# Attention projection stage scheduled in even slots, with the residual rows moved to the output stage

## What is computed

```python
x = L0_attn_x                                    # [16, 1024, 256]
mod = (silu(L0_c) @ L0_wmod).reshape(16, 6, 1, -1)
sa, ca, ga, sb, cb, gb = ...                     # shift, scale, gate, twice
h = _layernorm(x) * (1 + ca) + sa
x = x + ga * attn(h)       # attn(h) = h + softmax(mask(rope(q) @ rope(k).T / 4)) @ v @ Wo + bo
                           # q, k, v = (layernorm(h) * gamma + beta) @ W + b, 16 heads of 16
h = _layernorm(x) * (1 + cb) + sb
x = x + gb * ffn(h)        # 8 experts, 512 rows each, gathered and added back
```

## Time and profile before

| | |
|---|---|
| median of 3 runs | 3242.84 us (3241.46 to 3244.81) |
| the profiled execution: its own time | 3240.84 us |
| its span (first to last instruction) | 3239.1 us |
| projection stage | about 59 to 745 us of the span |
| scores and softmax | about 748 to 2612 us |
| output stage | about 2614 to 2894 us |
| busy: PE, DVE, ACT, POOL | 2817.5, 2278.7, 1765.1, 948.2 us |

### The profile page before, as it was taken

One profiled execution on the slowest core, in us unless ns is written; L12 is line 12 of the kernel. 1 busy time (PEld: TensorE's weight loads), 2 busy tenths in 40 slices (PEclk: granted clock), 3 DMA queues, 4 the chain that ended last, 5 costly groups with the idle time before them and its releaser, 6 DMA issues. The chain is left out here.

```text
span 3239.1 us, 48169 instructions
## 1 busy us (share of the span) xinstructions
PE 2817.5 (87%) x17587; PEld 1353.4 (42%) x17587; DVE 2278.7 (70%) x3286; ACT 1765.1 (54%) x3595; POOL 948.2 (29%) x1174
## 2 busy tenths in 40 slices
PE   1677777775999999999999999999999879975997
PEld 0333333331444444444444444444444347753664
DVE  4899999986777777777777777777777435553231
ACT  1455555550777777777777777777777721111111
POOL 2677777762112221121222211212222100003231
PEclk7888888885999999999999999999999989987999
DMA  2355555547344444445444444444444146663332
GB/s 77 127 192 192 192 192 192 191 156 169 71 97 96 92 93 91 99 100 100 97 94 92 94 91 100 100 100 97 91 94 93 42 188 258 258 230 102 79 103 54
DMA packets 173951, 402.96 MB, mean 124 GB/s; under 512 B 33147, under 2 KB 85792, under 8 KB 157107
## 3 DMA queue, kind: packets, MB, share of 16 engines
q1 hardware_dynamic: 167572, 391.36, 46.0%
q0 software_dynamic: 6144, 8.52, 1.5%
HBM read 240.65 MB, written 161.31 MB: 124 GB/s over the span
## 5 line engine op out<-in xcount | busy, mean ns | idle before, releaser
L962 DVE TENSOR_REDUCE mx<-ps 128x2 f32<-128x1024 f32 (+3 forms) x1216 | 1371.4, 1167 | 396.8 <-PE ps L1050 301.6
L1008 ACT ACTIVATE prob<-ps 128x512 f32<-128x512 f32 (+1 forms) x2560 | 1252.0, 560 | 538.4 <-PE ps L1068 529.7
L1043 PE MATMUL ps<-k_rows,q_rows 96*128 96x512 bf16 (+3 forms) x3072 | 911.2, 332 | 38.1 <-DMA k_rows<-k_parts 31.4
L1068 PE MATMUL ps<-q_rows,k_rows 99*128 99x512 bf16 (+3 forms) x3072 | 907.2, 328 | 14.7 <-ACT prob L1008 6.1
L901 POOL TENSOR_SCALAR_AFFINE_SELECT prob<-prob 128x512 f32<-128x512 f32 x512 | 320.0, 637 | 1451.3 <-ACT prob L1008 1451.3
L1087 PE MATMUL ps<-prob,v_rows 128*32 128x512 f32 (+3 forms) x6144 | 628.2, 496 | 0.0
L1068 PEld LDWEIGHTS ps<-q_rows,k_rows 99*128 99x128 bf16 x3072 | 273.1, 98 | 599.0 <-ACT prob L1008 360.2
L1043 PEld LDWEIGHTS ps<-k_rows,q_rows 96*128 96x128 bf16 x3072 | 290.2, 98 | 268.5 <-DVE mx L962 60.7
L1050 PE MATMUL ps<-mask_b,unit_b 128*128 128x128 bf16 (+2 forms) x1408 | 348.6, 248 | 0.0
L701 PE MATMUL ps<-x_t,w_all 128*128 128x512 f32 x512 | 233.2, 598 | 23.2 <-ACT x_t L582 23.2
L1087 PEld LDWEIGHTS ps<-prob,v_rows 128*32 128x32 f32 x6144 | 134.3, 108 | 245.8 <-ACT prob L1008 122.9
(11 more groups left out here) (154 smaller groups left out, 2745.3 us busy)
## 6 DMA issues: line engine op xcount, KB each, us to landing
k_rows<-k_parts SPq DMA_DIRECT2D x384, 128.0 KB, 7.4
v_ones<-v_st SPq DMA_DIRECT2D x64, 512.0 KB, 9.2
v_rows<-v_ones SPq DMA_DIRECT2D x64, 512.0 KB, 9.3
att<-o_sb SPq DMA_DIRECT2D x128, 256.0 KB, 3.2
att_b<-att SPq DMA_DIRECT2D x16, 2048.0 KB, 9.8
q_parts<-stage SPq DMA_DIRECT2D x128, 192.0 KB, 3.6
k_parts<-stage SPq DMA_DIRECT2D x128, 192.0 KB, 3.2
q_rows<-q_parts SPq DMA_DIRECT2D x64, 384.0 KB, 4.5
```

The lines of the kernel that those rows point to most:

```text
L962: dve.tensor_reduce(dst, src, AX.X, ALU.max).then_inc(a_free, 1)
L1008: nc.scalar.activation(prob[:, (g * NPC + i) % RING, h, 0:w], src, ACT.Exp).then_inc(exp_done, 1)
L1043: ins = pe.matmul(ps[:, at, col:col + w], q[0:ROWS, g, h, i * P:(i + 1) * P], k[0:ROWS, g, h, k0:k0 + w], start=(r == 0), stop=True, skip_ ...
L1068: ins = pe.matmul(ps[:, PS_B + bank(g, n), at:at + w], k[0:AUG, g, h, j * P:(j + 1) * P], q[0:AUG, g, h, q0:q0 + w], start=True, stop=True)
```

## The change

In the projection stage the two steps functions become one counter of even slots, s = -23 to 133, eight to a batch. `batch_at(s, lead)` says which tile or unit a piece of work is at. In slot s = 2n PE makes the product of unit n and in odd slots two tiles of v; DVE runs `multiply(n)` in slot 2n + 1, `combine(n)` in 2n + 2, behind `take_rest(n - 1)`; ACT runs `high(n)` in 2n + 3 and `middle(n)` in 2n + 5, POOL `low(n)` in 2n + 6. First norm, modulation and statistics of h go through at one tile a slot (ACT lead 17, POOL 16, DVE 15); the second norm is spread over six slots (`normed_in`). The shift sa is added by POOL behind its multiplication (new L630), but for batch 0, where DVE still adds it. `xin` and `mods_b` get three buffers, the first norm is made in place in `xin`, `h1` goes. L659, L662 and the store L403 go with their DRAM buffer. The factors `rsx` and `nmx` are kept for all 16 batches. In the output stage x is loaded again (`x_b`) with the a2 row, ACT makes the first norm once more (new L1184), two tiles ahead of its copy to `n_t`, POOL multiplies by a2 and adds x (new L1208, L1210). SP issues gate and bias row first, then attention output, x and a2 row.

```diff
+        RING = 3
...
+        START = -23
+        END = B * T + 6
...
+        def normed_in(s):
+            b, k = batch_at(s, 5)
+            if b is not None and k < 7:
+                yield ((0, 1), (2, 3), (), (4,), (5,), (6,), (7,))[k], b
+        def turned_in(s):
+            return normed_in(s - 1)
...
-            for b in range(2):
+            for b in range(RING + 1):
                 load(b)
-            store_residual(0)
-            load(2)
             for b in range(B):
-                if b + 1 < B:
-                    store_residual(b + 1)
-                if b + 3 < B:
-                    load(b + 3)
+                if b + RING + 1 < B:
+                    load(b + RING + 1)
                 store(b)
...
         def _(dve):
+            def slot(s):
+                n = (s - 1) // 2
+                if s % 2 == 1 and 0 <= n < B * NP:
+                    multiply(n)
+                n = (s - 2) // 2
+                if s % 2 == 0 and 0 <= n - 1 < B * NP:
+                    take_rest(n - 1)
+                if s % 2 == 0 and 0 <= n < B * NP:
+                    combine(n)
...
         def _(act):
+            def slot(s):
...
+                for tiles, b in turned_in(s - 1):
+                    for t in tiles:
+                        copy_x(b, t)
+                n = (s - 3) // 2
+                if s % 2 == 1 and 0 <= n < B * NP:
+                    high(n)
+                if s % 2 == 0 and 2 <= s <= B * T:
+                    for t in (s - 2, s - 1):
+                        copy_v(t // T, t % T)
+                n = (s - 5) // 2
+                if s % 2 == 1 and 0 <= n < B * NP:
+                    middle(n)
+                b, k = batch_at(s, 17)
+                if b is not None:
+                    first_norm(b, k)
+                for tiles, b in normed_in(s):
+                    for t in tiles:
+                        second_norm(b, t)
...
         def _(pool):
+            def modulate(b, t):
+                p, r = b % 2, b % RING
+                if t == 0:
+                    pool.wait_ge(mod_in[r], (b // RING + 1) * DMA)
+                reuse(pool, xt_done, (b - 2) * T + t + 1)
+                pool.wait_ge(h1_done, b * T + t + 1)
+                pool.tensor_tensor(h[:, p, t, :], xin[:, r, t, :], mods[:, r, M_CA1, :], ALU.mult).then_inc(h_mul, 1)
+                if b > 0:
                     pool.wait_ge(h_mul, b * T + t + 1)
-                    pool.tensor_tensor(h1[:, p, t, :], h1[:, p, t, :], mods[:, p, M_A2, :], ALU.mult).then_inc(r_mul, 1)
-                for t in tiles:
-                    pool.wait_ge(r_mul, b * T + t + 1)
-                    pool.tensor_tensor(h1[:, p, t, :], h1[:, p, t, :], xin[:, p, t, :], ALU.add).then_inc(r_done, 1)
+                    pool.tensor_tensor(h[:, p, t, :], h[:, p, t, :], mods[:, r, M_SA, :], ALU.add).then_inc(h_done, 1)
...
+            def slot(s):
+                b, k = batch_at(s, 16)
+                if b is not None:
+                    modulate(b, k)
+                n = (s - 6) // 2
+                if s % 2 == 0 and 0 <= n < B * NP:
+                    low(n)
...
-def phase3(nc, B, L, D, ps, ident, wo, ones3, mods_d, out_bias_d, resid_d, att_d, sum_d, out):
+def phase3(nc, x, ps, ident, wo, ones3, rsx, nmx, mods_d, out_bias_d, att_d, sum_d, out):
...
         def load(sp, b, p):
-            sp.dma_start(att[:, p], att_d[b].rearrange("g p t -> p g t")).then_inc(att_in[p], DMA)
-            sp.dma_start(res[:, p], resid_d[b]).then_inc(res_in[p], DMA)
             sp.dma_start(gate[:, p], mods_d[b, M_GA, :].partition_broadcast(P)).then_inc(small_in[p], DMA)
             sp.dma_start(ob[:, p], out_bias_d[b]).then_inc(small_in[p], DMA)
+            sp.dma_start(att[:, p], att_d[b].rearrange("g p t -> p g t")).then_inc(att_in[p], DMA)
+            reuse(sp, r_done, b * T - T)
+            sp.dma_start(xb[:, p], x[b].rearrange("(t p) d -> p t d", p=P)).then_inc(x_in[p], DMA)
+            sp.dma_start(a2[:, p], mods_d[b, M_A2, :].partition_broadcast(P)).then_inc(x_in[p], DMA)
...
             def work(b, half, p):
                 for t in range(T):
+                    n = b * T + t + 2
+                    if n < B * T:
+                        first_norm(n // T, n % T)
                     act.wait_ge(nt_done, b * T + t + 1)
...
+            def residual(b, t):
+                p = b % 2
+                pool.wait_ge(r_norm, b * T + t + 1)
+                if t == 0:
+                    pool.wait_ge(x_in[p], (b // 2 + 1) * 2 * DMA)
+                pool.tensor_tensor(res[:, p, t, :], res[:, p, t, :], a2[:, p, :], ALU.mult).then_inc(r_mul, 1)
+                pool.wait_ge(r_mul, b * T + t + 1)
+                pool.tensor_tensor(res[:, p, t, :], res[:, p, t, :], xb[:, p, t, :], ALU.add).then_inc(r_done, 1)
```

More of the change, by code:

```diff
@@ L330, in phase1 @@
     STORES = 2 * 2 * NG
+    RING = 3
     PS_X, PS_QK, PS_V = 0, 2, 6
-    assert L == 2 * W
+    assert L == 2 * W and T == 2 * NP
     with ExitStack() as ctx:
@@ L358, in phase1 @@
         v_st = sb("v_st", [P, 2, NG, T, NV], F32)
-        x_in, mod_in = pair("p1_x_in"), pair("p1_mod_in")
+        x_in = tuple(sem(f"p1_x_in{r}") for r in range(RING))
+        mod_in = tuple(sem(f"p1_mod_in{r}") for r in range(RING))
         stx_done, sth_done = sem("p1_stx"), sem("p1_sth")
@@ L549, in _ @@
-            invert_h(0)
-            steps(both)
-            take_rest(B * NP - 1)
+                b, k = batch_at(s, 18)
+                if b is not None and k == 0:
+                    invert_x(b)
+                b, k = batch_at(s, 6)
+                if b is not None and k == 0:
+                    invert_h(b)
+                b, k = batch_at(s, 15)
+                if b is not None:
+                    take_h(b, k)
+                    if k == T - 1:
+                        join_h(b)
@@ L553, in _ @@
+                b, k = batch_at(s, 23)
+                if b is not None and k < 4:
+                    take_x(b, k)
+                    if k == 3:
+                        join_x(b)
+            dve.memset(eps[:, :], EPS)
+            for s in range(START, END):
+                slot(s)
         @block.scalar
@@ L630, in _ @@
-            act.wait_ge(ones_set, 1)
-            root(0, 0, agx, agx_done, sdx_done)
-            first_norm(0, range(T))
-            root(1, 0, agx, agx_done, sdx_done)
-            root(0, 1, agh, agh_done, sdh_done)
-            second_norm(0, range(T))
-            for t in range(4):
-                copy_x(0, t)
-            steps(both)
-            high(B * NP - 1)
-            middle(B * NP - 1)
+            def slot(s):
+                b, k = batch_at(s, 19)
+                if b is not None and k == 0:
+                    root(b, 0, agx, agx_done, sdx_done)
+                b, k = batch_at(s, 7)
+                if b is not None and k == 0:
+                    root(b, 1, agh, agh_done, sdh_done)
+                for tiles, b in turned_in(s - 1):
[16 more added lines that the diff above has]
+                        second_norm(b, t)
@@ L642, in _ @@
+            act.wait_ge(ones_set, 1)
+            for s in range(START, END):
+                slot(s)
         @block.gpsimd
         def _(pool):
[L644 to L652 removed]
@@ L1189, in work @@
                 ins.then_inc(wg_done, 1)
-                dve.wait_ge(res_in[p], half * DMA + DMA)
                 for t in range(T + 2):
```

244 lines of the change are left out of this document (84 added, 160 removed).

## The result

The changed kernel took **3192.5 us** (median of 4 runs, 3186.1 to 3195.7) against 3243.0 (3241.5 to 3244.8): ratio 0.9841, 95% interval 0.9828 to 0.9854. It is 50 us faster where I forecast 16. The profiled execution took 3186.1 us, the lowest of the four runs, and its span is 3184.0.

The account below looks back on a forecast made before the run. DVE was taken to set the projection stage's pace, tied with ACT and POOL in a ring after the change; PE nearly fills the output stage. -35 + 19 + 1 = -15 from 3240.8, plus 2.0 for the median: 3227 us, range 3160 to 3252.

Parts of the forecast that it names:

- the ring: Projection stage: DVE, ACT and POOL wait on each other in a closed loop, 9.85 us for two slots, taken as 9.75.
- four pairs make 39.0 us a batch: Projection stage: four two-slot pairs at 9.75 us, 39.0 a batch against 40.9; 14 batches gain 27 us.
- its forecast: Projection stage in all: 27 + 12 - 4 = 35 us less.
- the last batches: Projection stage, last 16 slots: 26.6 us a batch; gain 12 us.
- in one pair of four DVE has less between and comes to L512 ahead of `low`, for about 0.5 less: Projection stage: one pair of four is about 0.5 us shorter, as DVE reaches L512 before POOL's `low`.
- Rival A: Projection stage: loop doesn't lock; 34.8 us a batch, 3168 us, or DVE alone sets pace, 30 to 32, 3115; chance 0.19.
- a small hole: Projection stage before the change: DVE waits for the first product at each batch's edge, 3.5 us each.
- the first product some 4 us later: Projection stage start: batch 0's work is spread over slots also carrying batches 1 and 2; costs 4 us.
- both are there at 13.8: Output stage: x and the a2 row land 13.8 us behind the store of x2 that frees the buffers.
- PE loses 1.3 to 1.4 us: Output stage: PE waits that long for n_t(6) in each of 14 batches, 19 us more.
- The slower rival, C: Output stage: x lands later still, each us costing 14; 3255 at 2 us, 3303 at worst; chance 0.20 with another rival.

Follow-up runs that it names:

- root_late: The changed kernel with ACT's two square roots of a slot at its end, behind casts and norms, in the projection stage; 3203.1 us.
- shift_dve_xf: x_first with the shift of all batches on DVE (old work, new order); 3199.9 us.
- resid_only_xf: The kernel before, old projection order and shift on DVE, with only the residual rows moved to the output stage, loads as in x_first; 3240.3 us, ratio 0.9992.
- x_first: The changed kernel with x and the a2 row issued ahead of the attention output in the output stage; 3133.4 us, ratio 0.9663.

## Why the prediction was right and wrong

**Right.** DVE sets the pace of the projection stage and PE has room (197.3 against 162.7 of 200 us). The DVE instructions with two inputs in SBUF are held behind whole POOL instructions, which the Trainium skill, "SBUF — State Buffer", section "Who interferes with whom", has as its rule. That it is mostly one POOL instruction at a time is what the rows show: L503 and L504 are at 1.2 us at the median, as the ring had them. In the output stage the wait is ACT's, at tile 6, for the row that comes last, and PE stands behind the copy. The signs of all terms but the start's are right.

**Wrong: "four pairs make 39.0 us a batch".** This is the step that failed. From the first store of v in batch 0 to that in batch 13 the stage took 436.9 us instead of 531.4, 94.5 less where thirteen batches at 1.9 make 25. That is 70 of the 78 us by which the projection stage beat its forecast; the start gave 12 more than forecast, the last batches and the stage's end some 3 less. I priced the closed ring correctly, 9.75 us for 9.6, and took it for all four pairs.

Within that step, the sentence that failed is "in one pair of four DVE has less between and comes to L512 ahead of `low`, for about 0.5 less". That pair exists, and it costs 3.7 less: root_late, whose ring closes in the other three pairs, has it at 5.9 us against 9.6 in every batch. When DVE comes first it isn't held once; the POOL instruction that stands beside it loses three turns, and `low` falls beside `multiply`, which it doesn't hold. I had counted two turns of POOL in that pair as in the others. Three closed pairs and this one make 34.8 us, so this accounts for 4.2 of the 4.9 us between my 39.0 and the 34.1 of the change. The other 0.7 is what I left out of the walk: ACT stands for the statistics twice a batch (5.9 and 3.4 us in the batch shown), after which POOL can get its tile so late that DVE is through.

Rival A had nearly the right number (34.8 us a batch at its first step), and I argued it down with two rows of the old order and one line of ACT's order. Its mechanism, two turns less in every pair, isn't what the traces show: three pairs keep theirs or something as long, and in one DVE isn't held at all.

**Wrong: what the old order cost.** I reckoned 40.9 as DVE's work plus a small hole. It is a stretch that counts and an edge of some 12 us in which DVE's work is free; the two runs in the old order show that taking out the rows gives 3 us (within the noise) and rows and shift together 11. The new order pays 40 us by itself, before the shift, and I gave it no term of its own.

**Start: "the first product some 4 us later".** The first store of v is 8.0 us earlier (122.4 for 130.4). The new order with the shift on DVE (shift_dve_xf) has it at 130.2, the old order without the rows (resid_only_xf) at 124.2. So the order does cost some 6 us at the start, near the 4 that I took, and what I left out is that the start also loses POOL's work on the rows (6 us) and DVE's shift (7).

**Output stage: "both are there at 13.8".** ACT's norm began at 15.4 on average. The a2 row is issued 3.4 us behind the store and lands 12.2 later at the median, 15.6 together. SP comes to it late, behind gate, bias and two large loads, where the residual rows' load went at 1.04; and x comes in pieces of 1 KB, for which I added 0.2. By the medians x is there at 2.8 + 11.5 = 14.3 us and the a2 row at 15.6, so most of the delay is the row's. Each number holds the queue ahead of it as well as its own pieces, and these weren't measured apart. The Trainium skill, "DMA: Bandwidth & Descriptors", section "Specifications", would have the pieces cost nothing; no run here held the two sizes apart either.

**"PE loses 1.3 to 1.4 us": it loses 3.8.** PE's wait is 2.6 us a batch (35.9 us in 14 times), and the clock behind it costs most of the rest: 16 groups of L1245 in the 14 batches take 1.5 to 2.1 us instead of 1.13, two of them in the batch shown. I had PE's 1.00 before me and took it to stay. The slower rival, C, was this very mechanism with its price of 14 us for each us; it happened, 1.6 us later than counted and dearer by the clock, and was covered by the other stage.

**Luck.** My wide range, 3160 to 3252, holds the 3192.5, but only since two errors offset each other: 78 us too little gain in the projection stage and 35 too little loss in the output stage. With the loads in a better order the same projection stage is at 3133, outside the range.

## What to carry to other kernels

Before a ring is priced, walk it through a whole batch with every other wait of its engines, since it costs only in the pairs in which it closes; ask above all who comes first in the pair with the least work. When a batch of a kernel is a stretch and an edge, find out in which of the two the work lies that is to be saved: here only the new order did away with the edge's cost. A load that moves behind a 2 MB one should be issued ahead of it if an in-order engine waits for it: that alone was worth 59 us here, and the change with it takes 3133 us.

## What was not expected of the hardware

The turns at the shared access aren't even. DVE stands behind one POOL instruction at a time (L503, L504 by 0.53 us), but the POOL multiplication that arrived at 423.87, inside an unheld L509, stood through L509, L503 and L504 and took 2.40 us instead of 0.73; the same length shows again in the run without `low` (its L627 at 300.23), and root_late has a POOL addition of 3.01 us of this kind in every batch. Where DVE had itself just been held (414.25), POOL's next instruction came in after L509 alone. Why the two cases differ isn't shown.

A short wait of PE can cost its clock. In the output stage 2.84 us of waiting were followed by two groups, almost 5 us, at the lower level (2.08 for 1.13 us each), while both batches shown of x_first, which has no such wait, are granted 1.00. It isn't the length of the wait alone: PE waits 1.6 to 3.5 us in each of 14 batches, in 11 of them one or two slower groups follow, and behind waits of 1.9, 2.2 and 2.6 us none does.

Still open: why the 120 additions of POOL are so nearly free (0.2 us of hold a pair) when the same instructions on DVE cost 66 us, beyond that DVE's wait for PE took some of it back.
